# GpSimd instead of ScalarE scales the residual rows at the start of attention_1, and the first output additions await their own rows only

## The reference

```python
def _L1_attn_ref(h, wq, bq, wk, bk, wv, bv, wo, bo, ln_g, ln_b):
    residual = h
    mu = jnp.mean(h, axis=-1, keepdims=True)
    var = jnp.mean(jnp.square(h - mu), axis=-1, keepdims=True)
    x = (h - mu) * jax.lax.rsqrt(var + EPS) * ln_g + ln_b
    ...
    q, k = rope(q), rope(k)
    attn = jnp.einsum('bihd,bjhd->bhij', q, k) * scale
    attn = jnp.where(causal[None, None], -jnp.inf, attn)
    attn = jax.nn.softmax(attn, axis=-1)
    o = jnp.einsum('bhij,bjhd->bihd', attn, v).reshape(b, s, N_HEADS * D_K)
    return o @ wo.T + bo + residual
...
x = x + _L1_attn_ref(_layernorm(x, axis=-1), ...)
```

## Time and profile before

| | us |
|---|---|
| median of 3 runs (lowest to highest) | 1025.12 (1023.92 to 1026.94) |
| the profiled execution, its own time | 1020.11 |
| its span, first to last instruction | 1018.3 |

### The profile page before, as it was taken

One profiled execution on the slowest core, in us unless ns is written; L12 is line 12 of the kernel. 1 busy time (PEld: TensorE's weight loads), 2 busy tenths in 40 slices (PEclk: granted clock), 3 DMA queues, 4 the chain that ended last, 5 costly groups with the idle time before them and its releaser, 6 DMA issues. The chain is left out here.

```text
span 1018.3 us, 20957 instructions
## 1 busy us (share of the span) xinstructions
PE 968.0 (95%) x7053; PEld 800.8 (79%) x7053; DVE 719.4 (71%) x2156; ACT 598.4 (59%) x1515; POOL 422.7 (42%) x412
## 2 busy tenths in 40 slices
PE   8899999999998998999998899999999998899988
PEld 6677778777876654877777788989888987788877
DVE  6777777777764568663368677778776786569994
ACT  2177777777775675232133877777777864335433
POOL 5767666767664301146532634445344431110000
PEclk9999999999999999999999999999999999999999
DMA  5360222122000200652230401101010100001111
GB/s 173 74 209 22 64 53 49 27 64 43 2 1 9 105 1 2 213 149 84 78 114 7 151 18 31 36 15 41 26 31 26 26 12 1 1 1 47 47 38 51
DMA packets 27640, 54.53 MB, mean 54 GB/s; under 512 B 4534, under 2 KB 14902, under 8 KB 25846
## 3 DMA queue, kind: packets, MB, share of 16 engines
q1 hardware_dynamic: 25350, 47.44, 16.3%
q0 software_dynamic: 2208, 6.03, 2.0%
HBM read 38.90 MB, written 6.16 MB: 44 GB/s over the span
## 5 line engine op out<-in xcount | busy, mean ns | idle before, releaser
L525 ACT ACTIVATE sb_a_P<-sb_a_nS,sb_a_nm 128x257 f32<-128x257 f32 x256 | 127.6, 507 | 86.3 <-DVE sb_a_nm L636 86.1
L435 POOL TENSOR_TENSOR sb_a_P<-sb_a_P,sb_a_rec 128x512 f32<-128x512 f32 x128 | 129.2, 1040 | 87.6 <-DVE sb_a_rec L647 87.5
L636 DVE CUSTOM_DVE_ANT_0 sb_a_nS<-a_pS,sb_a_mask,sb_a_nsink 128x256 f32<-128x256 f32 x256 | 109.3, 479 | 39.0 <-PE a_pS L784 39.0
L2229 ACT ACTIVATE sb_a_t<-a_pp,sb_a_w 64x512 f32<-64x512 f32 x128 | 87.6, 684 | 13.8 <-PE a_pp L144 6.0
L2301 DVE SCALAR_TENSOR_TENSOR sb_a_t<-a_pp,sb_a_w,sb_a_cs 128x512 f32<-128x512 f32 x64 | 47.8, 747 | 56.8 <-ACT sb_a_t L2229 56.8
L2153 POOL TENSOR_TENSOR sb_a_qT<-sb_a_t 128x512 f32<-128x512 f32 x32 | 41.2, 1288 | 108.9 <-DVE sb_a_t L2304 108.9
L144 PE MATMUL a_pp<-sb_x_high,sb_a_w_low 128*128 128x512 f32 x184 | 78.3, 425 | 7.7 <-DVE sb_a_P L591 4.8
L144 PE MATMUL a_pp<-sb_x_high,sb_a_w_high 128*128 128x512 f32 x184 | 72.8, 396 | 0.0
L144 PE MATMUL a_pp<-sb_x_low,sb_a_w_high 128*128 128x512 f32 x184 | 72.6, 395 | 0.0
L534 ACT COPY sb_xn<-a_pT 128x512 f32<-128x512 f32 x128 | 68.0, 583 | 1.9 <-PE a_pT L798 1.9
L798 PE MATMUL a_pT<-sb_ident,sb_a_P 128*128 128x128 f32 x512 | 68.2, 276 | 0.3 <-ACT sb_xn L534 0.3
(11 more groups left out here) (463 smaller groups left out, 2901.5 us busy)
## 6 DMA issues: line engine op xcount, KB each, us to landing
sb_a_kr<-sb_a_kall SPq DMA_DIRECT2D x28, 256.0 KB, 4.3
sb_f_w<-f_w SPq DMA_DIRECT2D x12, 384.0 KB, 2.9
sb_a_w<-a_w SPq DMA_DIRECT2D x16, 257.0 KB, 2.7
sb_m_egu<-m_egu SPq DMA_DIRECT2D x2, 1408.0 KB, 11.1
sb_a_w<-a_w SPq DMA_DIRECT2D x8, 259.0 KB, 2.7
sb_a_wo<-a_wo SPq DMA_DIRECT2D x8, 256.0 KB, 2.7
sb_a_wv<-a_wv SPq DMA_DIRECT2D x8, 256.0 KB, 2.7
sb_a_wo<-a_wo SPq DMA_DIRECT2D x16, 128.0 KB, 2.0
```

Source lines behind the costliest of these rows:

```text
L435: nc.gpsimd.tensor_tensor(part, part, rec[b % 2][:, h, :].rearrange("p (q o) -> p q o", o=1) .to_broadcast([P, 2, S]), ALU.mult).then_inc( ...
L525: out = nc.scalar.activation(Pm[b % 2][:, h, qt, 0:S + 1], nS[:, h, qt, 0:S + 1], ACT.Exp, bias=nm[b % 2][:, h, qt:qt + 1], scale=-1.0, ac ...
L636: out = nc.vector.tensor_tensor_reduce(nS[:, h, qt, 0:S], pS[h][:, qt * S:(qt + 1) * S], wmask[:, qt, :], -1.0, nsink[par][:, h:h + 1], AL ...
L2229: out = nc.scalar.activation(t2[n][a, :, :].rearrange("p b s -> p (b s)"), pp[n][b, :], ACT.Identity, bias=bias[b])
```

## The change

ScalarE's `grow` goes. GpSimd scales the eight tiles, one instruction each, behind its first four sums and ahead of the additions of `bo`. The output additions of head 0 that the opening step unrolls (units 0 and 1) await 2u + 2 additions of `bo` instead of the first one awaiting all eight; in the loop that follows, `before` is false, as it was.

```diff
@@ gpsimd
             project(0, 0)
             for t in range(NT):
+                pool.wait_ge(shifts, t // HALF + 1)
+                nc.gpsimd.tensor_scalar(k.x[:, t, :], k.x[:, t, :], grown[:, t:t + 1], shift[:, t:t + 1], ALU.mult, ALU.add)\
+                    .then_inc(grown_x, 1)
+            for t in range(NT):
                 pool.wait_ge(grown_x, t + 1)
                 nc.gpsimd.tensor_tensor(k.x[:, t, :], k.x[:, t, :], bo[:, :], ALU.add).then_inc(based, 1)
             heads(pool, step)
@@ scalar
-            def grow(c):
-
-                act.wait_ge(shifts, c // 2 + 1)
-                for t in (2 * c, 2 * c + 1):
-                    nc.scalar.activation(k.x[:, t, :], k.x[:, t, :], ACT.Identity, bias=shift[:, t:t + 1],
-                                         scale=grown[:, t:t + 1]).then_inc(grown_x, 1)
...
             for c in range(4):
                 swap(0, 0, c)
-                grow(c)
             heads(act, step)
@@ vector, add_y
-                if before(H, u, 1):
-                    dve.wait_ge(based, NT)
+                if before(H, u, A1_U):
+                    dve.wait_ge(based, 2 * u + 2)
```

## The result

The change makes the kernel slower: median 1031.65 us (1028.56 to 1033.02, 10 runs) against 1025.31 us (1023.43 to 1028.31, 10 runs), ratio 1.0058 with a 95% interval of 1.0046 to 1.0069, so 4.7 to 7.1 us. Forecast were 1029.9 us and a range of 1026.5 to 1032.5.

The account below looks back on a forecast made before the run. TensorE was taken to bound the heads. Opening -1.2, TensorE held back +4.4 and clock +1.6 made +4.8 us on the profiled 1020.11, so 1024.9, or 1029.9 us on the median; range 1026.5 to 1032.5.

Parts of the forecast that it names:

- The opening: Start of attention_1, up to the first scores: without ScalarE's scaling they come 1.2 us earlier, not 4.4.
- s: Time of one of GpSimd's eight scalings, start to start: 0.57 us, giving a delay of 8s - 1.36 = 3.2 us.
- the matrix-by-column row: GpSimd's `P * rec`, 1040 ns at 512 elements against 1290 for two matrices; basis for 0.57 us a scaling.
- the light 0.36: Rival, chance 0.18: a GpSimd scaling takes 0.36 us; TensorE gap 2.7 us with a clock fall, +3.0 us, 1028.1.
- the heavy 1.0: Rival, chance 0.10: a GpSimd scaling takes 1.0 us; +8.3 us, 1033.4.
- VectorE gets its turn at the next boundary: In GpSimd's series, head 1's `t2` gets in between two instructions, not at the series' end.
- toll: Two `t2` of head 1 each hold GpSimd's series 0.55 us, 1.1 in all; it may be zero.
- Where TensorE stops: Head 1's first values chunk: TensorE ends available work about 578.2 us, resumes at 582.6, a gap of 4.4 us.
- the forecast chain: Head 1, behind GpSimd's release: sum, ScalarE's swap, VectorE's `t1`, then TensorE resumes 3.61 us later.
- The clock: Behind TensorE's gap in head 1 the granted clock falls to half, costing 1.6 us (bounds 0 and 3.3).
- The waits: Head 0's first output additions await two, then four based rows instead of eight: worth 0, covered by over 7 us.
- It carries: In the heads, what TensorE is late by at head 1's first values chunk stays in the time to the end.

Follow-up runs that it names:

- The pauses: The changed kernel with each GpSimd addition of bo waiting for the one before it; ratio 1.0050 to the kernel before.
- the half scaling: The changed kernel with ScalarE scaling tiles 0 to 3 behind its second and fourth swaps, GpSimd only tiles 4 to 7; ratio 1.0015 to the kernel before.

## Why the prediction was right, point by point

The time was right and the main causes too: a short gain in the opening, then TensorE held back by GpSimd's longer queue, then a fall of the clock. Where and by what TensorE was held back was wrong, and that the size still came out right is luck.

- *The opening.* Right: swaps 2 and 3 at +4.3 and +6.2 (forecast +4.3 and +6.3), `t2` 1 ends at +4.76 as forecast, held by the first sum; 1.35 us won for 1.2.
- *s.* 0.57 forecast, 0.536 measured ((578.98 - 574.69) / 8): mis-sized by 0.3 us in all. The estimate from the matrix-by-column row was near; neither the light 0.36 nor the heavy 1.0 came. With s from 0.5 to 0.7 and the clock at 1.6 the prediction's own terms give 1029.4 to 1031.0; its 1028.8 to 1031.9 does not follow from them.
- *VectorE gets its turn at the next boundary.* Wrong for the additions: the step rested on a small copy, and here an instruction with two SBUF inputs waited from the first addition to the last. No toll was paid there (the forecast had 1.1 us). It is right for the scalings, at 0.44 us each for 0.55.
- *Where TensorE stops.* Forecast at the values chunk for 4.4 us; it stopped 4.85 us one chunk earlier, behind VectorE's blocked queue. ScalarE's swap 2 of head 1, which was to wait 4 us for GpSimd, found the sum ready; it was the exponential ahead of it that waited 4.78. The errors nearly cancel, by luck: the lockout costs 4.88 - 3.53 = 1.35 us, the missing toll and the lighter s give back 1.1 + 0.3. That is why the term came out right, 4.3 for 4.4. The pauses show the forecast chain by itself, with a gap of 5.06 at the values chunk.
- *The clock.* It fell; 2.1 us for 1.6, because the low stretch covered 4.2 us of work. The rival of light scaling counted on a fall behind a gap of 2.7 us; behind the 2.79 of the half scaling none came, so its 1.5 us for the clock are not borne out here.
- *The waits.* Worth nothing, as forecast; the first output addition comes at 594.38, 9.9 us behind the last addition of `bo`.
- *It carries.* The values chunk starts 4.98 us later than before, counted from the first swap, and the stage ends 4.99 later: what TensorE is late by there stays.

The sum was +4.8, the traces' stage has +5.0, the times 4.7 to 7.1. Whether anything beyond the stage's 5.0 is real is not settled.

## What to carry to other kernels

An engine that is 42% busy can have nothing to spare in one place: read the queue that the moved work joins, and what stands behind it, not the average. Work taken off the busiest engine of a ring helps only down to the next one in the ring; here, 1.3 of 4.4 us, and the same could be had by moving ScalarE's own instructions behind its swaps. A stall of TensorE can be paid for again by the clock: here it fell with gaps of 3.60, 4.85, 5.06 and 7.98 us and not with one of 2.79, though it did with 2.78 and 2.05 elsewhere in the program.

## What the runs showed of the hardware

A VectorE `tensor_tensor` with both inputs in SBUF did not get in between GpSimd additions of two 128x256 float32 tiles that followed each other without a pause: it took 5.39 to 5.42 us in five traces and 3.32 in the one where it began later in the series, each time until 0.54 or 0.55 us behind the last of them. Between GpSimd scalings with one such tile and two columns it got in, at 0.91 to 0.99 us against 0.68, and GpSimd took 0.44 us longer for each. With a wait between the additions it got in too, at the price of some 0.28 us for each of the seven pauses ((7.45 - 5.52) / 7, what `t2` held GpSimd for among it). A GpSimd scale-and-shift of 128x256 float32 took 0.54 us from start to start, an addition 0.69. What in the engines decides between the two was not tried.
